# LoRA/NF4 block gated by a binary-difference FFN, one core: two scan rings, split first product, refolded attention order, x1 sum by transfers

## What is computed

```python
xn = layernorm(x)
# branch 1: NF4 weights (16 levels x a scale per 64 inputs) with LoRA
attn = (lin(xn, q) + lin(xn, k) + lin(xn, v)) / 3
x1   = xn + lin(attn, o)
s    = x1 + lin(silu(lin(x1, gate)) * lin(x1, up), down)
# branch 2: W = mean + mean(|w - mean|) * sign(w - mean), for each of w1, w3, w2
f    = (silu(xn @ W1.T) * (xn @ W3.T)) @ W2.T
out  = x + s * silu(f)
```

## Time and profile before

| | |
|---|---|
| median of 3 runs | 665.79 us (662.33 to 666.79) |
| the profiled execution | 665.82 us, its span 664.0 us |
| PE, PEld busy | 558.6 us (84%), 447.9 us (67%) |
| DVE, ACT, POOL busy | 463.6 us (70%), 376.4 us (57%), 113.3 us (17%) |
| mean granted TensorE clock | 0.93 of full |
| chain that ended last | PE 45%, DVE 23%, ACT 14%, issue 10%, DMA 4%, POOL 2% |

### The profile page before, as it was taken

One profiled execution on the slowest core, in us unless ns is written; L12 is line 12 of the kernel. 1 busy time (PEld: TensorE's weight loads), 2 busy tenths in 40 slices (PEclk: granted clock), 3 DMA queues, 4 the chain that ended last, 5 costly groups with the idle time before them and its releaser, 6 DMA issues.

```text
span 664.0 us, 6488 instructions
## 1 busy us (share of the span) xinstructions
PE 558.6 (84%) x2304; PEld 447.9 (67%) x2304; DVE 463.6 (70%) x512; ACT 376.4 (57%) x494; POOL 113.3 (17%) x110
## 2 busy tenths in 40 slices
PE   1168688999999759888698479989899998999997
PEld 1155466888888647667586257767677886887886
DVE  6770548688887628772419947888888888988436
ACT  3866576657744634542237265587559667676310
POOL 0021323001300310022000930012004002101491
PEclk9778888999999888998988778979999999999999
DMA  9979531131820472045201362247217325623903
GB/s 339 401 272 391 209 117 63 61 126 41 178 84 0 80 216 84 0 105 107 52 1 33 74 122 60 61 91 155 59 33 138 80 57 122 123 59 80 221 1 126
DMA packets 37951, 76.72 MB, mean 116 GB/s; under 512 B 3872, under 2 KB 11936, under 8 KB 37920
## 3 DMA queue, kind: packets, MB, share of 16 engines
q1 hardware_dynamic: 24624, 57.57, 27.4%
q0 software_dynamic: 9216, 16.78, 14.2%
q10 hardware_dynamic: 4080, 1.97, 1.0%
HBM read 55.46 MB, written 4.06 MB: 90 GB/s over the span
## 4 chain that ended last, share of the span: by engine, by line
PE 45%; DVE 23%; ACT 14%; issue 10%; DMA 4%; POOL 2%; SPq 0%; ACTq 0%; DVEq 0%
PE down_ps L1278 17%; PE up_ps L1250 13%; PE gate_ps L1250 10%; DVE acc L1041 9%; ACT ramp L688 5%; POOL y L524 2%; PE side_ps L1303 2%; ACT sign_st L556 2%; PE down_ps L1356 2%; DVE up_ps L958 1%; DVE scan L863 1%; DMA sign<-sign_kept 1%; DMA scan<-in_mean 1%; ACT y_part L635 1%; DMA y<-y_part 1%
## 5 line engine op out<-in xcount | busy, mean ns | idle before, releaser
L1278 PE MATMUL down_ps<-h,dn 128*128 128x512 f32 x672 | 169.7, 410 | 18.9 <-ACT y_part L635 18.9
L1250 PE MATMUL up_ps<-xT,gu 128*128 128x512 f32 x672 | 167.4, 401 | 11.2 <-DVE h L963 11.1
L1250 PE MATMUL gate_ps<-xT,gu 128*128 128x512 f32 x672 | 168.0, 402 | 10.3 <-ACT silu_gate L617 7.2
L1278 PEld LDWEIGHTS down_ps<-h,dn 128*128 128x128 f32 x672 | 132.4, 199 | 52.2 <-ACT y_part L635 23.4
L1250 PEld LDWEIGHTS up_ps<-xT,gu 128*128 128x128 f32 x672 | 130.6, 195 | 41.6 <-issue 9.7
L1250 PEld LDWEIGHTS gate_ps<-xT,gu 128*128 128x128 f32 x672 | 129.8, 194 | 41.2 <-issue 9.3
L1041 DVE SCALAR_TENSOR_TENSOR acc<-ramp,acc 128x1536 f32<-128x1536 f32 x56 | 102.4, 1829 | 30.4 <-ACT ramp L688 29.7
L514 POOL DMA_DIRECT2D y<-y_part x64 | 55.5, 933 | 383.3 <-ACT y_part L635 383.2
L688 ACT ACTIVATE ramp<-codes,ramp_bias 128x1536 f32<-128x1536 uint8 x70 | 109.8, 1574 | 1.2 <-DVE acc L1041 1.2
L622 ACT ACTIVATE h<-up_ps 128x512 fp32r<-128x512 f32 x56 | 33.5, 597 | 112.7 <-DVE up_ps L955 60.0
L635 ACT ACTIVATE y_part<-down_ps 128x512 f32<-128x512 f32 x64 | 37.5, 596 | 45.5 <-PE down_ps L1278 33.1
(11 more groups left out here) (155 smaller groups left out, 508.0 us busy)
## 6 DMA issues: line engine op xcount, KB each, us to landing
y<-y_part POOLq DMA_DIRECT2D x64, 256.0 KB, 3.6
scale<-in_scales SPq DMA_DIRECT2D x28, 384.0 KB, 5.3
scan<-in_w SPq DMA_DIRECT2D x15, 512.0 KB, 7.4
scan<-in_mean SPq DMA_DIRECT2D x15, 512.0 KB, 8.3
base<-in_mean SPq DMA_DIRECT2D x10, 768.0 KB, 5.1
codes<-in_codes SPq DMA_DIRECT2D x14, 192.0 KB, 5.2
unit_st<-in_w SPq DMA_DIRECT2D x9, 256.0 KB, 7.3
unit_st<-in_mean SPq DMA_DIRECT2D x9, 256.0 KB, 7.8
```

What stands on the lines that cost most here:

```text
L1250: last = nc.tensor.matmul(ps[:, :], w[:, w_part, hc * P:(hc + 1) * P], xT[:, x_part, hc, th * HALF:(th + 1) * HALF], start=(hc == 0 and w_ ...
L1278: last = nc.tensor.matmul(down_ps[n % 3][:, :], dn[:, k % DN_SLOTS, w_part, hq * P:(hq + 1) * P], h_part(k, h_p, th), start=(k == ks[0] an ...
```

## The change

It touches four places:

- **Scan and first chunks.** The ring of 4 pairs becomes a ring of 5 w tiles and one of 3 mean tiles; a mean slot is free after DVE's subtraction. Eight of the 15 sums (`DVE_SUMS`) go from ACT (Abs) to DVE (`tensor_reduce` with absolute value). Sign slots go from 2 to 4. Chunk 0's gate product no longer waits for the coefficient: PE multiplies the mean part (`early_mean`) and the signs (`early_signs`) apart, and DVE adds coefficient times the second to the first (`early_sum`). Chunks 1 and 3 put their up product in the gate banks, so that two chunks' h are in flight. The order of ACT and DVE in the opening is rewritten.
- **Attention side.** `ATTN_COUNT` and `ATTN_SIDE` change; the split of MT moves into chunk 13. SP issues the loads of chunks 11 and 12 ahead of `A_down_raw`, which waits for the end of D2.
- **x1 stage.** Two of the NF4 steps stand ahead of the evictions of X. `T3` is split before the NF4 step of stage T. `y2` is made by one SP copy of the high part and four accumulating DMAs of the low part, behind D4's adds in POOL's list; `B_gu`'s up part and chunk 15's scale and codes come behind the copy in SP's list.
- **D4 and D5** (two-chunk groups) spread their ACT steps over the tiles.

```diff
+SCAN_W, SCAN_MEAN = 5, 3
+SIGN_SLOTS = 4
+DVE_SUMS = [3, 4, 6, 8, 9, 11, 13, 14]
...
-              "D2": (0, 4), 10: (0, 3), 11: (0, 2), 12: (0, 4), "D3": (0, 8), 13: (0, 5)}
+              "D2": (0, 4), 10: (0, 3), 11: (0, 3), 12: (0, 4), "D3": (0, 7), 13: (3, 0)}
...
@@ load_scan
-                if k >= SCAN_SLOTS:
-                    sp.wait_ge(scan_abs, k - SCAN_SLOTS + 1)
+                if k >= SCAN_MEAN:
+                    diff_wait(sp, k - SCAN_MEAN)
...
+                if k >= SCAN_W:
+                    sp.wait_ge(scan_sign, k - SCAN_W + 1)
+                    sum_wait(sp, k - SCAN_W)
...
@@ sync, x1 stage
-            load_scale(B0 + 1)
-            load_codes(B0 + 2)
+            sp.wait_ge(x1_lo, TT)
+            sp.wait_ge(MT_lo, HC)
+            sp.dma_start(y2[:, :, :], xT[:, HI, :, :].bitcast(f32)).then_inc(y2_copied, 16)
             sp.wait_ge(B_gu_hi, 1)
             sp.wait_ge(B_gu_lo, 1)
             sp.dma_start(B_gu_raw[0:ROWS3, 0:INTER], B_gu_in[:, UP, :]).then_inc(B_gu_loaded, 16)
+            load_scale(B0 + 1)
+            load_codes(B0 + 2)
@@ gpsimd
-            for g in range(1, FFN_GROUPS - 1):
+            for g in range(1, FFN_GROUPS):
                 y_add(g)
-            pool.wait_ge(x1_lo, TT)
+            pool.wait_ge(y2_copied, 16)
             for hc in range(HC):
-                nc.gpsimd.tensor_tensor(y2[:, hc, :], xT[:, HI, hc, :].bitcast(f32), xT[:, LO, hc, :].bitcast(f32),
-                                        ALU.add).then_inc(y2_ready, 1)
-            y_add(FFN_GROUPS - 1)
-            pool.wait_ge(y2_ready, HC)
+                pool.dma_start(y2[:, hc, :], xT[:, LO, hc, :].bitcast(f32), accum_op=ALU.add).then_inc(y2_ready, 16)
+            pool.wait_ge(y2_ready, 16 * HC)
@@ vector
+            def scan_sum(k):
+                kind, n = k // SCAN_TILES, k % SCAN_TILES
+                diff_wait(dve, k)
+                nc.vector.tensor_reduce(abs_sums[:, SUMS * kind + n:SUMS * kind + n + 1], scan_w[:, k % SCAN_W, :],
+                                        axis=AX.X, op=ALU.add, apply_absolute_value=True).then_inc(scan_abs_dve, 1)
+            def early_sum(th):
+                dve.wait_ge(gate_done, th + 1)
+                nc.vector.tensor_scalar(silu_buf(0, th), up_ps[th][:, :], coeff[:, GATE:GATE + 1], None, ALU.mult
+                                        ).then_inc(early_part, 1)
+                dve.wait_ge(early_part, th + 1)
+                nc.vector.tensor_tensor(early_ps[th][:, :], early_ps[th][:, :], silu_buf(0, th), ALU.add
+                                        ).then_inc(early_gate, 1)
@@ tensor
+            def early_mean(th):
+                pe.wait_ge(gu_lo, 1)
+                pe.wait_ge(xT_lo, TT // 2 * (th + 1))
+                for hc in range(HC):
+                    for w_part, x_part in PASSES:
+                        nc.tensor.matmul(early_ps[th][:, :], gu_weight(0, GATE)[:, w_part, hc * P:(hc + 1) * P],
...
+            def early_signs(th):
+                pe.wait_ge(unit_sign, 1)
...
+            early_mean(0)
+            early_mean(1)
+            early_signs(0)
             total(GATE)
-            for c in range(FIRST):
+            early_signs(1)
+            for c in range(1, FIRST):
                 project(c, GATE, 0)
```

More of the change, by code:

```diff
@@ L88, with scan_on_pool, pool_tiles, dve_tiles @@
             LORA_SIDE[ahead, 7 if ahead == "X" else 3 if type(ahead) is int else 6] = SPLIT_IN[stage]
+def scan_on_pool(k):
+    return k in POOL_SCAN
+def pool_tiles(k):
+    return sum(t <= k for t in POOL_SCAN)
+def dve_tiles(k):
+    return k + 1 - pool_tiles(k)
+def dve_sums(k):
+    return sum(t <= k for t in DVE_SUMS)
+def act_sums(k):
+    return k + 1 - dve_sums(k)
 def gu_count(k, kind=UP):
@@ L723, in down_stage, with MT_high @@
                         split(stage)
-                    else:
+                    elif len(GROUPS[g]) == 3:
                         steps(stage, 1, max(t - 1, 0), max(t, 1) if t < TT - 1 else None)
+                    elif t == 0:
+                        steps(stage, 1, 0, 1)
+                    elif t % 2 == 1:
+                        steps(stage, 1, t // 2, t // 2 + 1 if t < TT - 1 else None)
+            def MT_high():
+                for c in range(HC):
+                    act.wait_ge(side_used, SIDES - HC + c + 1)
+                    nc.scalar.activation(MT[:, HI, c, :], MT_acc[:, c, :], ACT.Copy).then_inc(MT_hi, 1)
             def A_down_high():
@@ L818, in _ @@
                     h_high(13, 1)
+                    steps("X", 0, 0, 2)
                     for t in range(TT):
@@ L832, in _ @@
                                              ).then_inc(T_hi, 1)
+                    steps("T", 1)
                 elif type(stage) is int:
@@ L837, in _ @@
                     if stage == 13:
-                        for c in range(HC):
-                            act.wait_ge(side_used, SIDES)
-                            nc.scalar.activation(MT[:, HI, c, :], MT_acc[:, c, :], ACT.Copy).then_inc(MT_hi, 1)
                         B_gu_scale(GATE)
@@ L1178, in _ @@
                     h_low(13, 1)
+                    steps("X", 0, 1, 2)
                     for t in range(TT):
@@ L1200, in _ @@
                         A_down_low()
-                    if stage == 13:
-                        for c in range(HC):
-                            dve.wait_ge(MT_hi, c + 1)
-                            nc.vector.tensor_tensor(MT[:, LO, c, :], MT_acc[:, c, :], MT[:, HI, c, :].bitcast(f32),
-                                                    ALU.subtract).then_inc(MT_lo, 1)
                 else:
```

275 lines of the change are left out of this document (185 added, 90 removed), and 6 rows, old and new, of the table ATTN_SIDE.

## The result

The change makes the kernel faster: 610.61 us (median of 4 runs, 610.07 to 611.89) against 666.29 us for the kernel before beside it. The ratio is 0.9176, 95% interval 0.9133 to 0.9218. The forecast was 599.0 us, in a range of 586 to 620; the forecast's own range, without the rivals, was 588 to 610. The profiled execution took 610.4 us, its span is 608.6 us, its mean granted clock 0.972.

What follows compares the result with a forecast made beforehand. PE's idle time (91.8 us) and low clock in the first three stages were taken to bound the kernel; 85.0 + 195.6 + 48.5 + 268.1 = 597.2, with 1.8 around it 599 us; own range 588 to 610, asked-for range 586 to 620.

Steps and rivals of the forecast that it cites:

- Opening, 85.0: From the start to D0: D0 was to start at 85.0 us instead of 109.64, ends 80 and 97.
- (a): Opening: PE waits for the up coefficient, whose last tile's mean is issued late; 2.2 us.
- (c): Opening: PE waits for the down coefficient, behind chunk 2's up and, on DVE, h of chunk 1; 2.3 us.
- (b): Opening: PE waits for chunk 0's up split, which stands behind the up coefficient; 1.2 us.
- (d): Opening: D0 waits for three down units' splits on DVE, 2.1 us longer than chunk 3's up product.
- D0 to X, 195.6: From D0 to X: idle time and slow stretches go, less new waits; 195.6 us instead of 222, ends 190 and 209.
- The new waits: D0 to X: fold after chunk 8's gate 1.0, D2's second fold 1.5, fold after chunk 12's gate 1.5, MT's split 0.5.
- the 2 us that the signs gave for a fold: D0 to X: the trace after was to show folds waiting under 2 us each.
- X to chunk 14's rank part, 48.5: From X's start to chunk 14's rank part: 48.5 us instead of 67.2, the middle of 45.7 (400 GB/s) and 51 (half).
- Rival 1: x1 stage: slow copy blocks SP's queue, B_gu's load, ACT, T3 and PE; slow end +21, about 617 us; chance 0.14.
- Rival 2: Opening stays bound by its loads through the mean ring of 3; D0 at 97, 611 us; chance 0.13.
- rival 3: D0 to X: folds find new waits as DVE is later with each step; +11, 612 us; chance 0.12.

Runs made afterwards that it cites:

- the run with the early coefficient: Kernel after with scan rings of 4 and 4, tile 13's sum on ACT, and DVE taking the down coefficient before h of chunk 1's second half: 611.75 us.
- The two runs on the kernel before: Kernel before with SP's loads of chunks 11, 12 and attention half 7 ahead of A_down: 652.58 us; the same plus the new ATTN_COUNT and ATTN_SIDE: 640.15 us.
- the run with the late copy: Kernel after with the copy of x1 into y2 issued only after D4's eight adds landed, behind the B_gu, scale and codes loads: 604.43 us.

## Why the prediction was right, and where it was off

- **What bounds the kernel, stage by stage**: right. All of the gain lies in the three stages named, and the last is 1.4 us longer than before.
- **Opening, 85.0**: +3.1. PE's start, the gate coefficient and chunk 1's product came within 0.2 us; PE was ready for the coefficient 1 us before the 30.8 forecast, and waited. DVE's 128x1024 reduce took 1.21 us (1.2 taken), also beside POOL: the one at 50.72 us took 1.22 beside POOL's subtraction at 50.25, where DVE's split with two inputs at 59.15, beside POOL's at 59.11, took 1.82 instead of 0.68. Waits (a) and (c) were 1.2 us too small each, and "3.0 for POOL's subtractions and for a slower clock" was too little, as the clock alone took 4.4 (1.4 and 3.0). Waits (b) and (d) did not show, which fits PE being slow ahead of them; in the run with the early coefficient, where PE is not slow, (d) shows at 4.67 us (2.1 forecast). So the places in the sum were right, and their sizes partly cancel.
- **D0 to X, 195.6**: 194.7. The new waits were 1.07, 0.97, 2.80 and 0.69 us for 1.0, 1.5, 1.5 and 0.5 forecast; the third is above the 2 us that the signs gave for a fold. That the term came out within 0.9 us has some luck in it: in seven of the ten variants of the kernel after, 1.4 to 1.7 us more go to the clock behind that wait. The two runs on the kernel before show the causes: chunk 11's signs, then the order of the folds.
- **X to chunk 14's rank part, 48.5**: this is the term that was mis-sized; it measured 59.3. The step that failed is "POOL's adds run at once, but ACT still evicts behind steps and splits": it has no wait of ACT for a free slot. The adds were issued at once, but landed after 11.1 us and not after 3.6, because I looked only at what the copy does to B_gu behind it, not to the adds beside it. The path up to it held: D4 started 24.8 us after X's start (24.5), x1 was split at 29.0 (28.7), and T was through at 43.5 (41.5). But ACT's turn for B_gu came at 53.0 instead of 39.8, and ACT's waits for slots, which the sum put at nothing, are 12.8 of these 13.2 us. From that turn to the rank part it took 6.2 us, 5.9 forecast. The copy's rate, on which I spent the bounds, was the lower of the two values that I took the middle of: 2048 KB in 10.5 us from issue, 200 GB/s by that, and B_gu landed 45.7 us after X's start (45 at half rate). It set nothing, since ACT did not wait for B_gu. Moving the copy takes 7.8 us off the stage.
- The page DMA: Bandwidth & Descriptors of the Trainium skill (section Where 436 GB/s comes from) has transfers from SBUF to SBUF bound by the fabric at 435 GB/s. This copy did not reach it: it took 8.5 us for 2048 KB in the run with the late copy, where it has the quietest place, 247 GB/s from issue to landing, with 377 GB/s in the best window of 2 us there.
- **Rival 1** (the x1 sum by transfers is slow) named the right place, at half its price (+10.8 where its slow end was +21), by another way than it said: not B_gu behind the copy in SP's queue, but D4's adds beside the copy. **Rival 2** and **rival 3** did not happen. Their forecasts, 611 and 612 us, are as near to the measured time as can be, which says nothing for them.
- **The number**: 610.61 us is 0.6 us outside the forecast's own range, and inside the range asked for because that was widened for rivals 1 to 3. The forecast sum of the gain was 67 us, the measured gain 55.7.

## What to carry to other kernels

A large transfer is not free because its result is needed late: look at what else is in flight at the moment at which it is issued, and who waits for that; issue it after the small urgent ones. Before an engine's list is rearranged, read SP's: the cheapest gain here was a few loads moved past a wait in it. And a wait with low clock behind it is worth only as much as the next engine's list allows: with the early coefficient both came back at D0, and nothing was won. Last, run the same code twice before you believe 2 us in a profile of it.
